# The fourth layer's sixteen input sums move to the first two steps of a chunk, and the layer follows 19 steps behind instead of 25

## The reference: what is computed

```
x = x + L0(x, cond)      # x + x @ (base + low-rank matrix made from cond)
x = x + L1(x, cond)      # tanh(x @ W_ih.T + (cond @ W_hh.T + b_hh + b_ih))
x = x + L2(x, cond)      # LSTM, h0 = cond, c0 = 0
x = x + L3(x, cond)      # LSTM, h0 = cond, c0 = 0, other weights

# an LSTM, for each batch row, over the 2048 tokens t in order:
a = x[t] @ Wx + b + h @ Wh            # 2048 columns: i, f, o, g
c = sigmoid(f) * c + sigmoid(i) * tanh(g)
h = sigmoid(o) * tanh(c)              # h is the layer's output for t
```

## Time and profile before

| | us |
|---|---|
| time, median of 3 runs | 12079.07 (12078.11 to 12079.57) |
| the profiled execution's own time | 12079.69 |
| its span in the profile | 12077.9 |
| PE busy | 11989.9 (99%) |
| DVE busy | 7443.5 (62%) |
| ACT busy | 3043.5 (25%) |
| POOL busy | 1415.3 (12%) |

### The profile page before, as it was taken

The page is one execution under the profiler, slowest core; times in us unless marked ns, Lnnn a source line. Parts: engine busy times, 40 slices in busy tenths (PEclk is TensorE's granted clock), DMA queues, the critical chain, the costliest instruction groups (busy, mean ns, idle before and its releaser), DMA issues.

```text
span 12077.9 us, 683462 instructions
## 1 busy us (share of the span) xinstructions
PE 11989.9 (99%) x430906; PEld 4551.0 (38%) x168762; DVE 7443.5 (62%) x34041; ACT 3043.5 (25%) x20594; POOL 1415.3 (12%) x5261
## 2 busy tenths in 40 slices
PE   9999999999999999999999999999999999999998
PEld 6433333343333343333343333343333343333333
DVE  2566666666666666666666666666666666666664
ACT  1222222222222222222222222222222222222221
POOL 4011111111111111111111111111111111111110
PEclk9999999999999999999999999999999999999999
DMA  4000000000000000000000000000000000000000
GB/s 162 26 6 6 6 6 6 6 6 6 6 6 6 6 6 6 6 6 6 6 6 6 6 6 6 6 6 6 6 6 6 6 6 6 6 6 6 6 6 5
DMA packets 375968, 123.85 MB, mean 10 GB/s; under 512 B 350158, under 2 KB 358350, under 8 KB 372956
## 3 DMA queue, kind: packets, MB, share of 16 engines
q1 hardware_dynamic: 363212, 62.00, 2.8%
q0 software_dynamic: 3504, 11.56, 0.3%
q10 hardware_dynamic: 6240, 6.29, 0.2%
HBM read 62.98 MB, written 16.78 MB: 7 GB/s over the span
## 4 chain that ended last, share of the span: by engine, by line
PE 98%; DVE 1%; issue 0%; ACT 0%; DMA 0%; SPq 0%; DVEq 0%; POOLq 0%; POOL 0%
PE bank L80 89%; PE bank L822 7%; PE bank L489 1%; PE bank L502 1%; DVE gates_t L1002 0%; PE bank L455 0%; DVE pre L1007 0%; DMA wx<-in_Wx 0%; ACT tanh_c L899 0%; ACT sig L894 0%; DVE prod L1014 0%; DVE state L1025 0%; DVE state L1021 0%; DVE state L1028 0%; DVE gc L1017 0%
## 5 line engine op out<-in xcount | busy, mean ns | idle before, releaser
L80 PE MATMUL bank<-wh,state 128*12 128x256 bf16 x393216 | 11459.6, 273 | 51.9 <-DVE state L1028 39.1
L80 PEld LDWEIGHTS bank<-wh,state 128*12 128x12 bf16 x131072 | 3406.8, 88 | 6486.8 <-issue 6130.7
L1002 DVE STREAM_TRANSPOSE gates_t<-bank 128x256 f32<-128x256 f32 x4096 | 1844.0, 450 | 1562.9 <-PE bank L80 1560.4
L894 ACT ACTIVATE sig<-pre 128x16 f32<-128x16 f32 x4096 | 885.7, 216 | 7069.3 <-DVE pre L1007 7069.3
L1007 DVE TENSOR_REDUCE pre<-gates_t 128x24 f32<-128x96 f32 x4096 | 1340.4, 327 | 143.1 <-issue 2.3
L1014 DVE TENSOR_TENSOR prod<-sig,gc 128x16 f32<-128x16 f32 x4096 | 718.8, 175 | 1130.1 <-ACT gc L895 1032.4
L1021 DVE TENSOR_TENSOR state<-sig,tanh_c 128x8 f32<-128x8 f32 x4096 | 690.4, 169 | 1124.8 <-ACT tanh_c L899 1124.8
L899 ACT ACTIVATE tanh_c<-gc 128x8 f32<-128x8 f32 x4096 | 854.1, 209 | 1709.8 <-DVE gc L1017 1709.8
L929 POOL TENSOR_TENSOR x<-x1r,state 128x8 f32<-128x8 f32 x2048 | 432.7, 211 | 5466.6 <-DVE state L1028 5466.6
L929 POOL TENSOR_TENSOR y<-x,state 128x8 f32<-128x8 f32 x2048 | 432.6, 211 | 5053.9 <-DVE state L1028 5053.9
L822 PE MATMUL bank<-wx,x 128*32 128x128 f32 x16384 | 817.5, 273 | 4.9 <-DMA wx<-in_Wx 4.9
(11 more groups left out here) (109 smaller groups left out, 1665.4 us busy)
## 6 DMA issues: line engine op xcount, KB each, us to landing
w<-in_w SPq DMA_DIRECT2D x8, 2048.0 KB, 18.6
out<-y_rows SPq DMA_DIRECT2D x1024, 8.0 KB, 1.9
wx<-in_x SPq DMA_DIRECT2D x16, 512.0 KB, 6.6
x1p<-x_t_all SPq DMA_DIRECT2D x128, 64.0 KB, 2.7
x1r<-x_t_all SPq DMA_DIRECT2D x128, 64.0 KB, 2.6
x_t_all<-wx ACTq DMA_DIRECT2D x6, 1024.0 KB, 4.9
wx<-in_Wh POOLq DMA_DIRECT2D x8, 512.0 KB, 4.4
wx<-in_Wh POOLq DMA_DIRECT2D x16, 256.0 KB, 5.9
```

The source lines that it names most:

```text
L80: return pe.add_instruction(mybir.InstMatmult(name=nc.get_next_instruction_name(), engine=mybir.EngineType.PE, ins=[pe.lower_ap(moving), p ...
L894: act.activation(sig[l][:, 0:2 * HB], pre[l][:, 0:2 * HB], ACT.Sigmoid)
L1002: dve.transpose(gates_t[l][:, :, NS * NB:], gates[l][:, 0:NMS * C].rearrange("p (m c) -> p m c", c=C)).then_inc(s["trans"], 1)
```

## The change

`sums` now goes by the table `SUMS`: L3's sixteen sums stand eight each in steps 0 and 1, L2's stand two each in steps 2 and 3 and one each in steps 4 to 15. `LAG` becomes 19. A helper `share` splits the sums of a step between its layers, the first half (rounded up) after the first layer's products; the quarters to turn and to add the bias to are split in the same way. `turn_rows` moves from step 10 to step 4 and to the step's last layer. In the first chunk the sixteen tile blocks stand one each in steps 0 to 11 and two each in steps 12 and 13, and SP loads the last quarter of `wx3` before it stores the last tile.

```diff
--- before.py
+++ after.py
@@ -561,7 +561,12 @@
 
 NFRONT = NTILE - 2
 
-LAG = CH + CH // 2 + 1
+
+SUMS = ((0, 0, 2, 2) + (1,) * 12, (8, 8) + (0,) * 14)
+
+LAG = CH + 2 + 1
+
+ROWS_AT = LAG - CH + 1
 
 BODY = 20
 
@@ -617,11 +622,9 @@
 
     def sums(self, s):
 
-
-        if s < CH // 2:
-            found = [(L3, -1, 2 * s + k) for k in range(2)]
-        else:
-            found = [(L2, 1 + (2 * s - CH + k + AHEAD) // CH, (2 * s + k + AHEAD) % CH) for k in range(2)]
+        first = [sum(SUMS[l][:s]) for l in (L2, L3)]
+        found = [(L3, -1, first[L3] + k) for k in range(SUMS[L3][s])]
+        found += [(L2, 1 + n // CH, n % CH) for n in range(AHEAD + first[L2], AHEAD + first[L2] + SUMS[L2][s])]
         return [(l, d, *divmod(n, NH)) for l, d, n in found if self.number is None or 0 <= self.number + d < NCH]
 
     def done_before(self, s):
@@ -630,6 +633,12 @@
             return [x[:3] for x in self.sums(s - 1) if x[3] == NH - 1]
         before = Chunk(self.v, self.i - 1)
         return [(l, d - 1, q) for l, d, q, h in before.sums(CH - 1) if h == NH - 1]
+
+    def share(self, items, l, s):
+
+        layers = self.layers(s)
+        first = -(-len(items) // len(layers))
+        return items[:first] if l == layers[0] else items[first:]
 
 
 def layers_and_recurrence(nc, ins, keep, turn, pool_stream, cut_done, x1_dram, out):
@@ -677,9 +686,11 @@
         x1_aside = {NFRONT: keep["wx3"][:, 0, :], NFRONT + 1: keep["area"][0]}
         x1_aside = {u: to.rearrange("p (h n) -> p h n", h=NH) for u, to in x1_aside.items()}
 
-        def slot_of(s):
-
-            return NFRONT + s // (2 * NH), s // NH % 2, s % NH
+        def blocks_of(s):
+
+
+            units = (s,) if s < 12 else (2 * s - 12, 2 * s - 11) if s < 14 else ()
+            return [(NFRONT + n // (2 * NH), n // NH % 2, n % NH) for n in units]
 
         names = ("mm", "xp", "trans", "pre", "pre_o", "g", "prod", "c", "tanh", "h", "r1", "r2", "res",
                  "proj", "turn", "ready")
@@ -748,8 +759,9 @@
                     load_wx3(0)
                     sp.wait_ge(tiles.s_x0, NH * NTILE)
                     load_wx3(2)
+                    sp.wait_ge(tiles.s_x1, NH * NTILE)
+                    load_wx3(3)
                     store_x1(NFRONT + 1)
-                    load_wx3(3)
                     sp.wait_ge(tiles.s_store, NTILE * DMA)
 
                 def emit(t):
@@ -838,16 +850,15 @@
                         for l in layers:
                             pe.wait_ge(S[l]["r2"], t.count(l, s))
                             matmuls(l).then_inc(S[l]["mm"], 1)
-
-                            for x in sums[l:l + 1] if len(layers) == 2 else sums:
+                            for x in t.share(sums, l, s):
                                 project(x[0], t, *x[1:])
                         if t.number == 0:
-                            first_layers(s)
+                            for x in blocks_of(s):
+                                first_layers(*x)
                         elif len(layers) == 1:
                             keep_warm()
 
-                def first_layers(s):
-                    u, which, ho = slot_of(s)
+                def first_layers(u, which, ho):
                     to = sets[1][ho]
                     if which == 0:
 
@@ -898,13 +909,13 @@
                             act.wait_ge(S[l]["c"], n)
                             act.activation(tanh_c[l][:, :], gc[l][:, HB:], ACT.Tanh).then_inc(S[l]["tanh"], 1)
                         if t.number == 0:
-                            u, which, h = slot_of(s)
-                            if which:
-                                tiles.tanh(act, u, h, sets[1][h])
-                            elif u + 1 < NTILE:
-
-                                act.wait_ge(tiles.s_store, u * DMA)
-                                turn.copy_block(act, u + 1, h, spare)
+                            for u, which, h in blocks_of(s):
+                                if which:
+                                    tiles.tanh(act, u, h, sets[1][h])
+                                elif u + 1 < NTILE:
+
+                                    act.wait_ge(tiles.s_store, u * DMA)
+                                    turn.copy_block(act, u + 1, h, spare)
 
                 for u in range(NFRONT):
 
@@ -948,9 +959,8 @@
                                 pool.wait_ge(s_x1r[t.slot()], (t.half() + 1) * DMA)
 
                             residual(l, t, s)
-                            if l == layers[0]:
-                                for x in t.done_before(s):
-                                    add_bias(x[0], t, *x[1:])
+                            for x in t.share(t.done_before(s), l, s):
+                                add_bias(x[0], t, *x[1:])
 
                 pool_stream(pool)
                 pool.sem_inc(S[L2]["res"], 1)
@@ -979,11 +989,10 @@
 
                 def between(l, t, s):
 
-                    if l == t.layers(s)[0]:
-                        for x in t.done_before(s):
-                            turn_quarter(x[0], t, *x[1:])
-                        if t.rows and s == LAG - CH + 1:
-                            turn_rows(t, -2)
+                    for x in t.share(t.done_before(s), l, s):
+                        turn_quarter(x[0], t, *x[1:])
+                    if t.rows and s == ROWS_AT and l == t.layers(s)[-1]:
+                        turn_rows(t, -2)
 
                 def emit(t):
                     for step in range(t.steps):
@@ -1028,11 +1037,11 @@
                             dve.tensor_tensor(part(st, 2), part(st, 1), upper(part(st, 1)),
                                               ALU.subtract).then_inc(s["r2"], 1)
                         if t.number == 0:
-                            u, which, h = slot_of(step)
-                            if which:
-                                tiles.sum1(dve, u, h, sets[1][h], x1_aside[u])
-                            else:
-                                tiles.sum0(dve, u, h, sets[1][h])
+                            for u, which, h in blocks_of(step):
+                                if which:
+                                    tiles.sum1(dve, u, h, sets[1][h], x1_aside[u])
+                                else:
+                                    tiles.sum0(dve, u, h, sets[1][h])
                             if step == CH - 1:
 
                                 dve.wait_ge(tiles.s_x1, NH * NTILE)
```

## The result

The changed kernel takes 12451.61 us (median of 4 runs, 12450.06 to 12453.11) against 12078.59 us before: a ratio of 1.0308, with a 95% interval of 1.0296 to 1.032. It is 373 us slower. The forecast was 12433 us, 18.6 us too low. The profiled execution took 12450.06 us, with a span of 12448.2 us.

The account below looks back on a forecast made before the run. PE's own work was taken to bound the kernel. The terms, 373 + 9 + 0 + 7 - 5 - 30.5 = +353 us on 12079.7 us, gave 12433 us, range 12390 to 12540 us.

Parts of the forecast that it names:

- (a): Steps 0 and 1: PE waits twice a chunk for a turned quarter, 1.48 us each, +373 us.
- (b): Steps 4 to 15: one sum serves two half steps, cover just fits the chain, late weight load costs +9 us.
- rival 4: Steps 4 to 15: late weight load costs its full 0.07 us, +214 in place of +9, 12638 us; chance 0.07.
- (c): POOL's bias additions, `turn_rows` and the store after it move within the chunk, priced at 0.
- (d): Chunk 0: PE idles in steps 14 and 15, +5.2 us, and the clock may fall once, some 2 us.
- (e): Chunk 1: 89.5 us after, 94.9 before, -5.4 us, if the wait for the `wx3` weights goes.
- (f): The end: 25 steps of L3 alone become 19, together -30.5 us.
- Rival 1: Steps 0 and 1: the waits for turned quarters don't arise, -23 us, 12057 us; chance 0.04.
- Rival 2: Steps 0 and 1: one of the two waits in a chunk is hidden, +166 us, 12246 us; chance 0.04.
- Rival 3: Steps 0 and 1: the clock falls in the waits, once in every chunk +216 us, 12650 us; chance 0.05.

Follow-up runs that it names:

- the first experiment: The changed kernel, but DVE turns a quarter (and POOL adds its bias) in the half step right after its completion; 12072.22 us, ratio 0.9993.
- the second experiment: The changed kernel, but all quarters completed in a step are turned in the next step's first part; 12256.45 us, ratio 1.0147.

## Why the prediction was right

(a) The two waits. Forecast 1.48 us each; the trace has 1.47 us from the products' end to the sum. A step 1 is 9.99 us against the 9.9 forecast, and 6.99 where the waits are taken away, so a wait costs 1.50 us all told; the four sums behind a wait take 0.90 us and not 0.87, since their first weight load is laid bare. With 126 chunks that is 378 us where 373 stood, 5 us more. Halving the waits gave back half. The count was 255 against 254 (one lies ahead of the loop, as before).

(b) Steps 4 to 15. This is the term that was mis-sized: +9 us was taken, and the runs show 23 to 26 (what these steps take beyond their medians, without the delays over 1 us, goes from 4.2 to 26.9 us; in the experiment with thick cover 26 us went). That the cover "just fits" was right: the median step is 5.46 us, PE's work alone, so the weight load that starts right before its product costs nothing, and rival 4 is out. The 9 us stood for that load, so their cause was wrong as well as their size. What I missed is that the chain isn't always 2.81 us. Now and then DVE begins an instruction late, as here in the changed kernel, where L1011 comes 0.71 us after the last work and not some 0.35 as in the earlier trace rows:

```profile
526.31 0.34 PEld L80 LDWEIGHTS bank<-wh,state 128*12 128x12 bf16 x8 [0.32 <-DVE state L1037]
...
526.96 0.45 DVE L1011 STREAM_TRANSPOSE gates_t<-bank 128x256 f32<-128x256 f32 x1 [0.71 <-PE bank L80]
...
528.95 0.40 PE L834 MATMUL bank<-wx,x1p 128*32 128x128 f32 x8
...
529.28 0.17 DVE L1037 TENSOR_TENSOR state<-state 128x8 f32<-128x8 f32 x1
...
529.50 1.71 PE L80 MATMUL bank<-wh,state 128*12 128x256 bf16 x56 [0.16 <-DVE state L1037]
```

The products were due at 528.95 + 0.22 = 529.17 and came at 529.50, 0.33 us late. The old cover of 3.06 us swallowed all but 0.1 us of such a delay. In the changed kernel 81 steps are 0.2 to 0.4 us over their median, 26.6 us in all, against 5 steps and 1.2 us before; 68 of them, with 22.0 us, are among steps 4 to 15, and the other 13 are a step 1, where PE waits for DVE anyway. The dummies that restored the cover removed them, which is what shows the cause. The prediction said of rival 4 that the margin is "less than any delay in the records"; the delays were in the trace of before and I should have counted them there.

(c) POOL, `turn_rows` and the stores at 0: nothing in the waits of PE speaks against it, and step 4, which now has `turn_rows`, takes 5.46 us in the mean, as its neighbours do in the median.

(d), (e) Chunks 0 and 1. +4.6 and -3.0 us against +7 and -5.4, so +1.6 together as forecast. Part of that is the loss of clock, which (d) had in chunk 0 with 2 us: the clock did fall, but in chunk 1's first step. In the timeline of PE, with the clock of that stretch from the view by windows:

```profile
370.50 0.39 PE L834 MATMUL bank<-wx,x1p 128*32 128x128 f32 x8
373.32 4.30 PE L80 MATMUL bank<-wh,state 128*12 128x256 bf16 x96 [2.42 <-DVE state L1037]
377.44 1.92 PE L834 MATMUL bank<-wx,x 128*32 128x128 f32 x64
```

```profile
373.10:376.30 3.20, 2.98 (x60) 0.71 (x24) 0.65 (x2) 0.00 (x0) 0.21 (x1) 0.50 0.30 35
```

After 2.42 us of idle time the clock was at its lower level of 1.2 GHz, and the products took 4.12 us to the next run and not 2.62, 1.5 us more. The wait for `wx3` is gone: the sums start right behind the products.

(f) The end: -31.7 us against -30.5.

The sum. In chunks 2 to 127 the +400.4 us are 378.4 by the medians, 30.2 more in delays of under 1 us, and 8.2 less in delays of over 1 us, most of them where the loop goes back (19.7 us before, 11.5 after). No term had the last, and it was luck that it stood against the two terms that came out too small: kernels of these experiments with the same six rounds lose 10 to 22 us to such delays. The forecast for the spans was +353 us and they differ by 370.3.

The rivals. Rival 1 was what the change would have been with the turning in its right place, and the first experiment made it: 12072 us where 12057 was forecast for it; the delays of (b) are most of the difference. Rival 2 is the second experiment, 12256 us where 12246 stood. Rival 3 did not come: between the first and the last step the clock fell once, at 373 us, though PE stood for 1.47 us twice in each chunk. The granted clock of nearly the whole stretch with both layers (the column after POOL's):

```profile
480.00:12340.00 11860.00, 11507.43 (x418900) 4174.10 (x161044) 7257.46 (x33367) 2942.73 (x20150) 1265.44 (x5031) 1.00 0.03 6
```

The rule on cycling through PSUM banks in the Trainium skill ("TensorE: Matmul & The Clock Gate", the section on psum-queue depth-cycling) so does not describe pauses of this length at this distance.

## What to carry to other kernels

When work is gathered into fewer steps, ask of each buffer pair in it when the engine that empties it gets its turn: two banks are only double buffering if the emptying stands, in its engine's own order, ahead of anything that waits for the producer. A cover that just fits the median chain pays for every late instruction; count the late ones in the old trace and price them before thinning the cover. Here, moving one DVE instruction by half a step was worth 379 us, more than ten times what the shorter lag gains. And even with the instruction in its place the change is hardly worth having: of the 35 us that the shorter lag gains, the thin cover takes some 26 back.

## What the runs showed of the hardware

DVE starts an instruction 0.17 to 0.39 us late at regular places in its instruction stream. Counting DVE's records between such delays (semaphore waits and register instructions counted too, and only starts that come late against the usual time behind the instruction before), 126 of 131 distances in the changed kernel and 85 of 90 in the kernel before are whole multiples of 128. The others are five of 808 and five of 174, one for each time that the loop goes back. It looks like a cost of fetching DVE's instructions; no run varied their number, so that cause stays open. In the experiment with twice the code in the loop's body the steps that PE lost to delays of 0.2 to 0.4 us fell from 73 to 58.

PE's dummy products, issued in a written-out stretch of code, stood still for 2.75 us in one run and 2.60 us in another with nothing to wait for that the profile shows. In the first the clock fell after it, in the second it stayed up. So dummies that are there in the code don't by that alone keep PE busy; look in the trace whether they were issued in time.
